# First feed-forward layer: silu on ScalarE instead of tanh there and a finishing product on VectorE

## The chip, the core and the metric

The kernel runs on one core of one Trainium2 chip, as one launch. The metric is the device time in microseconds of that core. The core's engines are TensorE (PE in the profile; PEld is its loading of weights), VectorE (DVE), ScalarE (ACT), GpSimd (POOL) and SyncE (SP), each with its own instruction stream. They wait for each other through semaphores. PSUM is the memory that TensorE writes its products to, in banks of 128 partitions by 512 fp32 numbers.

## The reference, cut to what matters

The input x has 4 sequences of 1024 tokens with 256 features. Six layers are applied in turn, each added to x:

```
x = x + 0.5 * L0_ffn(layernorm(x))
x = x + L0_attn(layernorm(x))
x = x + 0.5 * L0_ffn(layernorm(x))      # the same weights again
x = x + 0.5 * L1_ffn(layernorm(x))      # a mixture of experts
x = x + L1_attn(layernorm(x))
x = x + 0.5 * L1_ffn(layernorm(x))

def L0_ffn(x):                           # wq_*: whole numbers, s_*: one scale per row
    gate = silu(x @ ((wq_gate - 128) * s_gate[:, None]).T)     # 256 -> 704
    up   =      x @ ((wq_up   - 128) * s_up[:, None]).T        # 256 -> 704
    return (gate * up) @ ((wq_down - 128) * s_down[:, None]).T # 704 -> 256
```

silu(g) is g / (1 + exp(-g)), which is the same as 0.5 g (1 + tanh(g / 2)). The change touches `L0_ffn` alone, which runs twice.

## The kernel before, in words

The program is a row of phases, one function each: `prepare_phase` loads and turns the weights of the first layer, `ffn0_phase` ("f1_") is the first feed-forward layer, `attention_phase` ("a2_") the first attention, `ffn0_phase` ("f3_") the feed-forward layer again, and then come `mixture_phase`, `attention_phase` and `mixture_phase` once more. Between two phases there is a barrier of all engines: each engine enters the next block when all have left the one before.

`ffn0_phase` works through 8 chunks c of 512 tokens (4 tiles of 128). The hidden 704 features are 6 blocks j: five of 128 and a last one, j = 5, of 64. The gate and the up product of a block go to PSUM tiles `gate` and `up` with two banks each; block n = 6c + j uses bank j % 2, so block n can begin only when block n - 2 has let go of the bank. In the last block both halves fit into one bank: one group of four matmuls with the weights `ctT` gives the gate's 64 rows on partitions 0 to 63 of the gate's bank and the up product's 64 rows on partitions 64 to 127.

Inputs and hidden values are split into a high and a low fp16 part (`xh`, `xl`, and `hh`, `hl`), so each product is two fp16 matmuls. What each engine does, in the order in which it is written:

- TensorE: `gate_up(c, j)` (line 385) is 4 gate matmuls of 512 columns and then 4 up matmuls, all recorded on line 395. Behind block 1 stands `turn(c + 1)`, 8 transposes of the next chunk's normalised x, and behind each of blocks 1 to 4 one `down_proj(c - 1, i)`, 12 matmuls of 256 columns (line 407), which need all six `hl` of the chunk before. `gate_up` waits before its first gate matmul for `h_ready` of block n - 2, that is until VectorE has written `hT` of that block; with j = 0 it also waits for `xT_ready` of its chunk.
- ScalarE: `tanh(c, j)` (line 454, recorded on line 459) reads the gate's bank and writes tanh of half the scaled gate to `silu`. Then `upper_part(c, j - 1)` (line 452) copies `hT` of the block before to fp16 `hh`. Behind block 2 stands `keep_xT(c + 1)`, two copies to `xh` (line 447).
- VectorE: `gated(c, j)` (line 504, recorded on 507) makes `silu2` = (silu + 1) * gate, reading the gate's bank again. `hidden(c, j)` (line 510, recorded on 517) makes `hT` = silu2 * scale * up. In the last block the up rows are read from the gate's bank. The trace gives `silu2` the name `f_silu` as well. Between these stand the pieces of the work for the other chunks: the means (lines 487, 490, 493) and the normalising (501) of chunk c + 2, `lower_part` (524) for `xl` of chunk c + 1, `residual` (531) for the down product of chunk c - 1, `statistics` (536), which waits until GpSimd has added that tile to x, and `aggregate` (540).
- GpSimd: `add(c - 1, i)` (line 427) adds the finished tile to x, and `hl` = hT - hh (line 435) follows for every block. `hidden` of block n waits until `hl` of block n - 2 is written, since `hT` has two buffers.

In the names of the trace the first letter is the phase's, `f_` for both feed-forward phases. At the end of the phase the last chunk's four `down_proj` follow with nothing beside them.

## Time and profile before

| | |
|---|---|
| median of 3 runs | 2764.04 us (2758.51 to 2764.95) |
| the profiled execution | 2757.35 us, of which its span is 2755.6 us |
| TensorE, VectorE, ScalarE, GpSimd busy | 2581.0, 1872.7, 1269.7, 788.3 us |
| first feed-forward phase, first gate matmul to the last down matmul's end | 42.95 to 190.25 us of the span |
| second feed-forward phase, the same | 1142.47 to 1292.85 us |

The span runs from the first to the last instruction of the profiled execution; 1.75 us of the execution lie around it. Busy time is the time in which at least one instruction of the engine was under way. TensorE is busy 94% of the span, but a busy share is a mean over phases with different limits, so the change is read from the two feed-forward phases alone. Matmuls overlap: one of 512 columns is recorded with 0.38 us at the full clock while the next starts 0.22 us after it. So what a wait costs is read from start to start.

### The profile page before, as it was taken

How to read it: one execution, taken by the hardware profiler on the slowest of the kernel's cores; microseconds unless marked ns; L12 is line 12 of the kernel's file. 1: busy time of each engine (PE TensorE's matmuls, PEld its weight loads, DVE VectorE, ACT ScalarE, POOL GpSimd, SP SyncE). 2: the span in 40 equal slices, each digit the busy share in tenths (PEclk: the TensorE clock that was granted, in tenths of full speed). 3: DMA queues.
4: the chain of work that ended last, by engine and by line, in shares of the span. 5: the costliest groups of instructions: out<-in, count | busy, mean ns of one | idle time of the engine just before them, and what ended most of it. 6: DMA issues, size and time to landing. Idle time of an engine off the chain costs nothing. (4 is left out here: it accounts for less than half of the span.)

```text
span 2755.6 us, 38804 instructions
## 1 busy us (share of the span) xinstructions
PE 2581.0 (94%) x14106; PEld 1255.9 (46%) x14106; DVE 1872.7 (68%) x4022; ACT 1269.7 (46%) x1936; POOL 788.3 (29%) x760
## 2 busy tenths in 40 slices
PE   5987999999999999897999998899999999899998
PEld 3543333333333332354565665445544554555665
DVE  7868888788787885585664335787777776466334
ACT  4431666566566667543212322365454556321321
POOL 2545214132141300155424541311121110234441
PEclk8997999999999999899999999999999999999999
DMA  4004430331303400001303654634223440311565
GB/s 126 1 17 92 64 52 19 58 56 21 58 24 53 64 1 2 1 1 55 109 20 101 158 119 114 118 50 71 48 54 57 65 59 2 115 35 35 139 156 161
DMA packets 162592, 175.76 MB, mean 64 GB/s; under 512 B 19090, under 2 KB 135762, under 8 KB 162258
## 3 DMA queue, kind: packets, MB, share of 16 engines
q1 hardware_dynamic: 146948, 152.57, 25.4%
q0 software_dynamic: 12416, 17.84, 3.9%
q10 hardware_dynamic: 3040, 2.88, 0.4%
q8 instruction: 113, 1.85, 0.3%
q14 instruction: 75, 0.61, 0.1%
HBM read 116.32 MB, written 56.13 MB: 63 GB/s over the span
## 5 line engine op out<-in xcount | busy, mean ns | idle before, releaser
L1862 DVE TENSOR_REDUCE a_mx<-a_bank 128x1 f32<-128x512 f32 (+3 forms) x1792 | 1034.6, 626 | 241.7 <-PE a_bank L1595 173.1
L1730 ACT ACTIVATE a_E<-a_bank 128x1024 f32<-128x1024 f32 (+3 forms) x896 | 796.2, 931 | 401.5 <-PE a_bank L1653 273.7
L1595 PE MATMUL a_bank<-a_KT,a_QT 96*128 96x512 bf16 (+4 forms) x1792 | 572.3, 368 | 25.6 <-DVE a_mx L1862 15.2
L1653 PE MATMUL a_bank<-a_QT,a_KT 99*128 99x512 bf16 (+4 forms) x1792 | 505.1, 357 | 3.9 <-DMA a_QT<-a_mT 1.8
L1668 PE MATMUL a_bank<-a_E,a_Vg 128*32 128x512 f32 (+3 forms) x3584 | 437.3, 560 | 0.7 <-ACT a_E L1730 0.7
L1595 PEld LDWEIGHTS a_bank<-a_KT,a_QT 96*128 96x128 bf16 (+1 forms) x1792 | 152.0, 98 | 490.1 <-DVE a_mx L1862 307.5
L1653 PEld LDWEIGHTS a_bank<-a_QT,a_KT 99*128 99x128 bf16 (+1 forms) x1792 | 169.6, 98 | 173.5 <-ACT a_E L1730 31.4
L435 POOL TENSOR_TENSOR f_hl<-f_hT,f_hh 128x512 f16<-128x512 f32 x96 | 110.9, 1156 | 340.3 <-ACT f_hh L452 340.3
L903 PE MATMUL d_bank<-wdT,d_hT 128*128 128x256 f32 (+1 forms) x768 | 192.4, 393 | 4.2 <-DVE d_hT L1100 4.2
L1014 ACT ACTIVATE d_silu<-d_bank 128x512 f32<-128x512 f32 x96 | 57.1, 595 | 270.0 <-PE d_bank L888 270.0
L903 PEld LDWEIGHTS d_bank<-wdT,d_hT 128*128 128x128 f32 (+1 forms) x768 | 140.2, 191 | 63.2 <-issue 43.6
L888 PE MATMUL d_bank<-d_xT,wgT 128*128 128x512 f32 x320 | 162.6, 632 | 4.4 <-DMA wdT<-in_L_ffn_sw_down 4.4
L780 POOL DMA_INDIRECT acc<-d_ys,d_index x64 | 101.2, 1582 | 192.9 <-DVE d_ys L1216 119.6
L888 PE MATMUL d_bank<-d_xT,wuT 128*128 128x512 f32 x320 | 152.4, 599 | 0.0
L1530 POOL TENSOR_TENSOR a_Z<-a_Z,a_turns 128x512 f32<-128x512 f32 x24 | 30.5, 1270 | 414.6 <-DVE a_R L1811 414.6
L1668 PEld LDWEIGHTS a_bank<-a_E,a_Vg 128*32 128x32 f32 x3584 | 70.7, 108 | 139.9 <-issue 120.2
L1095 DVE SCALAR_TENSOR_TENSOR d_silu<-d_silu,d_bank 128x512 f32<-128x512 f32 x96 | 65.3, 680 | 98.9 <-ACT d_silu L1014 98.9
L1618 PE MATMUL a_bank<-a_xT,wqkvT 128*128 128x512 f32 x256 | 125.1, 621 | 2.0 <-DVE a_mx L1862 2.0
L790 POOL TENSOR_SCALAR d_xn<-x,mv,d_both 128x256 f32<-128x256 f32 x48 | 60.0, 1258 | 229.0 <-DVE d_shift L1237 150.8
L1108 DVE SCALAR_TENSOR_TENSOR x<-d_bank,d_hgate,x 128x256 f32<-128x256 f32 x64 | 30.9, 484 | 121.2 <-PE d_bank L903 121.1
L1598 PE MATMUL a_bank<-a_masks,ident_b 128*128 128x128 bf16 x512 | 112.3, 222 | 0.0
L459 ACT ACTIVATE f_silu<-f_gate,hscale 128x512 f32<-128x512 f32 x96 | 64.4, 683 | 103.8 <-PE f_gate L395 103.8
(235 smaller groups left out, 3633.9 us busy)
## 6 DMA issues: line engine op xcount, KB each, us to landing
parts<-a_parts SPq DMA_DIRECT2D x64, 384.0 KB, 2.6
a_QT<-parts SPq DMA_DIRECT2D x180, 128.0 KB, 5.9
a_KT<-parts SPq DMA_DIRECT2D x180, 128.0 KB, 9.1
d_wgu<-in_L_ffn_w_gate SPq DMA_DIRECT2D x64, 176.0 KB
d_wgu<-in_L_ffn_w_up SPq DMA_DIRECT2D x64, 176.0 KB
d_wd<-in_L_ffn_w_down SPq DMA_DIRECT2D x64, 176.0 KB
normalised<-d_xn SPq DMA_DIRECT2D x8, 1152.0 KB, 4.7
acc<-d_zero SPq DMA_DIRECT2D x2, 4224.0 KB, 16.4
```

What stands on the lines that cost most here:

```text
L435: nc.gpsimd.tensor_tensor(hl[0:r, c % 2, j, :], hT[0:r, j % 2, :], hh[0:r, c % 2, j, :], ALU.subtract).then_inc(hl_ready, 1)
L780: nc.gpsimd.indirect_dma_start(out=acc, out_offset=bass.IndirectOffsetOnAxis(ap=index[:, e:e + 1], axis=0), in_=ys[:, e % 2, :], in_offset ...
L888: last = nc.tensor.matmul(out, w[:, k, cols], xT[:, k, c * CW:(c + 1) * CW], start=(k == 0), stop=(k == KC - 1))
L903: last = nc.tensor.matmul(bank[:, down_bank(c, i), 0:D], hT[0:r, c % 2, j, i * P:(i + 1) * P], core.wdT[0:r, j, :], start=(j == 0), stop=( ...
L1095: nc.vector.scalar_tensor_tensor(out=silu2[0:r, j % 2, :], in0=silu[0:r, j % 2, :], scalar=1.0, in1=bank[0:r, acc_bank(n), :], op0=ALU.add ...
L1595: last = nc.tensor.matmul(out[:, 0:w], QT[0:W, h, qt * P:(qt + 1) * P], KT[0:W, h, kh * HALF:kh * HALF + w], start=True, stop=not diag)
L1598: last = nc.tensor.matmul(out[:, w - P:w], ident_b[:], masks[:, 0, :], start=False, stop=True)
L1618: last = nc.tensor.matmul(out, core.wqkvT[:, k, cols], xT[:, k, half * HALF:(half + 1) * HALF], start=(k == 0), stop=(k == KC - 1))
L1653: last = nc.tensor.matmul(out, KT[:, h, kt * P:(kt + 1) * P], QT[:, h, half * HALF + c0:(half + 1) * HALF], start=True, stop=not diag)
L1668: last = nc.tensor.matmul(bank[VW * j:VW * (j + 1), 4, c0:HALF], Vg[:, G % NG, kt, VS * j:VS * j + VW], E[:, u % 2, j, c0:HALF], start=fir ...
L1730: nc.scalar.activation(E[:, u % 2, 2 * pair:2 * pair + 2, c0:HALF], bank[:, 2 * pair:2 * pair + 2, c0:HALF], ACT.Exp).then_inc(exps, 1)
L1862: nc.vector.tensor_reduce(mx[:, x[1] // C % 2, j, qt, kh:kh + 1], out[:, 0:w], AX.X, ALU.max).then_inc(freed_dve, 1)
```

## The change

ScalarE no longer computes tanh of half the gate. It computes silu of the whole gate, with the scale that the weights ask for, and writes it to the same tile. VectorE's `gated` goes, with its tile `silu2` and its semaphore. What was `tanh` on ScalarE is now called `gated`, and `hidden` multiplies silu, up and one scale. The scales prepared once in `prepare_phase` change with that.

On TensorE the wait is moved and split. Before its gate matmuls a block waited for VectorE to have written `hT` of block n - 2. Now the gate matmuls wait for ScalarE to have read the gate's bank (`silu_ready` of block n - 2), and the up matmuls for `h_ready` of block n - 2. For j = 1, where block n - 2 is the last block of the chunk before and has its up rows in the gate's bank, the gate matmuls still wait for `h_ready`.

```diff
--- before.py
+++ after.py
@@ -295,9 +295,8 @@
                 statistics(1)
                 dve.wait_ge(s_in, 16 * 4)
                 for r, j in ((P, slice(0, FB - 1)), (hid(FB - 1), slice(FB - 1, FB))):
-                    nc.vector.tensor_scalar(core.hscale[0:r, j, 0], sg[0:r, j], 0.5 / LIFT, None, ALU.mult)
-                    nc.vector.scalar_tensor_tensor(out=core.hscale[0:r, j, 1], in0=sg[0:r, j], scalar=HLIFT / LIFT ** 2,
-                                                   in1=su[0:r, j], op0=ALU.mult, op1=ALU.mult).then_inc(scaled, 1)
+                    nc.vector.tensor_scalar(core.hscale[0:r, j, 0], sg[0:r, j], 1.0 / LIFT, None, ALU.mult)
+                    nc.vector.tensor_scalar(core.hscale[0:r, j, 1], su[0:r, j], 2.0 * HLIFT / LIFT, None, ALU.mult).then_inc(scaled, 1)
                 dve.wait_ge(r_in, START + 16 * 3)
                 nc.vector.tensor_tensor(prod[:], srows[:, 0], srows[:, 1], ALU.mult).then_inc(scaled, 1)
                 dve.wait_ge(scaled, START + 3)
@@ -351,7 +350,6 @@
         xh = sb(tag + "xh", [P, 2, KC, CW], F16)
         xl = sb(tag + "xl", [P, 2, KC, CW], F16)
         silu = sb(tag + "silu", [P, 2, CW])
-        silu2 = sb(tag + "silu2", [P, 2, CW])
         hT = sb(tag + "hT", [P, 2, CW])
         hh = sb(tag + "hh", [P, 2, FB, CW], F16)
         hl = sb(tag + "hl", [P, 2, FB, CW], F16)
@@ -363,8 +361,8 @@
         gate = ps(tag + "gate", [P, 2, CW])
         up = ps(tag + "up", [P, 2, CW])
         down = ps(tag + "down", [P, 2, 512])
-        names = ("root scales normed turned xh_ready xT_ready gate_s up_s silu_s silu2_s h hh_s hl_s down_s out_s x_done stats meaned")
-        (root, scales, normed, turned, xh_ready, xT_ready, gate_ready, up_ready, silu_ready, silu2_s, h_ready, hh_ready, hl_ready, down_ready,
+        names = ("root scales normed turned xh_ready xT_ready gate_s up_s silu_s h hh_s hl_s down_s out_s x_done stats meaned")
+        (root, scales, normed, turned, xh_ready, xT_ready, gate_ready, up_ready, silu_ready, h_ready, hh_ready, hl_ready, down_ready,
          out_s, x_done, stats, meaned) = (sem(tag + n) for n in names.split())
         ident = core.const("ident")
 
@@ -386,10 +384,13 @@
                     n, s = c * FB + j, c % 2
                     if j == 0:
                         pe.wait_ge(xT_ready, START + c * 2 + 2)
-                    if n > 1:
-                        pe.wait_ge(h_ready, START + n - 1)
                     for w, acc in ((core.cgT, gate), (core.cuT, up)) if j < FB - 1 else ((core.ctT, gate),):
                         cols = slice(j * P, (j + 1) * P) if j < FB - 1 else slice(0, P)
+                        if n > 1:
+                            if acc is gate and j != 1:
+                                pe.wait_ge(silu_ready, START + n - 1)
+                            else:
+                                pe.wait_ge(h_ready, START + n - 1)
                         for k in range(KC):
                             for part in (xh, xl):
                                 last = nc.tensor.matmul(acc[:, j % 2, :], w[:, k, cols], part[:, s, k, :],
@@ -451,18 +452,18 @@
                     act.wait_ge(h_ready, START + c * FB + j + 1)
                     nc.scalar.activation(hh[0:r, c % 2, j, :], hT[0:r, j % 2, :], ACT.Copy).then_inc(hh_ready, 1)
 
-                def tanh(c, j):
+                def gated(c, j):
                     n, r = c * FB + j, hid(j)
                     act.wait_ge(gate_ready, START + n + 1)
                     if n > 1:
                         act.wait_ge(h_ready, START + n - 1)
-                    nc.scalar.activation(silu[0:r, j % 2, :], gate[0:r, j % 2, :], ACT.Tanh,
+                    nc.scalar.activation(silu[0:r, j % 2, :], gate[0:r, j % 2, :], ACT.Silu,
                                          scale=core.hscale[0:r, j, 0:1]).then_inc(silu_ready, 1)
 
                 keep_xT(0)
                 for c in range(NCH):
                     for j in range(FB):
-                        tanh(c, j)
+                        gated(c, j)
                         if j:
                             upper_part(c, j - 1)
                         if j == 2 and c + 1 < NCH:
@@ -501,20 +502,14 @@
                     nc.vector.tensor_scalar(xn[:, i, :], core.x[:, t, :], mean[:, i:i + 1],
                                             core.rstd[:, t:t + 1], ALU.subtract, ALU.mult).then_inc(normed, 1)
 
-                def gated(c, j):
+                def hidden(c, j):
                     n, r = c * FB + j, hid(j)
                     dve.wait_ge(silu_ready, START + n + 1)
-                    nc.vector.scalar_tensor_tensor(out=silu2[0:r, j % 2, :], in0=silu[0:r, j % 2, :], scalar=1.0,
-                                                   in1=gate[0:r, j % 2, :], op0=ALU.add, op1=ALU.mult).then_inc(silu2_s, 1)
-
-                def hidden(c, j):
-                    n, r = c * FB + j, hid(j)
-                    dve.wait_ge(silu2_s, START + n + 1)
                     if j < FB - 1:
                         dve.wait_ge(up_ready, START + c * (FB - 1) + j + 1)
                     if n > 1:
                         dve.wait_ge(hl_ready, START + n - 1)
-                    nc.vector.scalar_tensor_tensor(out=hT[0:r, j % 2, :], in0=silu2[0:r, j % 2, :], scalar=core.hscale[0:r, j, 1:2],
+                    nc.vector.scalar_tensor_tensor(out=hT[0:r, j % 2, :], in0=silu[0:r, j % 2, :], scalar=core.hscale[0:r, j, 1:2],
                                                    in1=up[:, j % 2, :] if j < FB - 1 else gate[FR:P, j % 2, :],
                                                    op0=ALU.mult, op1=ALU.mult).then_inc(h_ready, 1)
 
@@ -553,7 +548,6 @@
                 for c in range(NCH):
                     more = c + 2 < NCH
                     for j in range(FB):
-                        gated(c, j)
                         if more and j <= 1:
                             mean_step(c + 2, j)
                         if j >= 2 and c:
```

What this does on VectorE is shown at the passage from one chunk to the next, from `hidden` of a chunk's last block (`64x512`) to `hidden` of the next chunk's second block. Before:

```order
L536 BN_STATS f_bn<-x 128x6 [waits f1_x_done]
L517 SCALAR_TENSOR_TENSOR f_hT<-f_silu,hscale,f_gate 64x512 [waits f1_hl_s,f1_silu2_s]
L501 TENSOR_SCALAR f_xn<-x,f_mean,rstd 128x256
L540 BN_AGGR mv<-f_bn 128x2 [waits f1_stats] x4
L507 SCALAR_TENSOR_TENSOR f_silu<-f_silu,f_gate 128x512 [waits f1_silu_s]
L487 TENSOR_REDUCE f_sums<-x 128x64 [waits f1_normed]
L517 SCALAR_TENSOR_TENSOR f_hT<-f_silu,hscale,f_up 128x512 [waits f1_hl_s,f1_up_s,f1_silu2_s]
L507 SCALAR_TENSOR_TENSOR f_silu<-f_silu,f_gate 128x512 [waits f1_silu_s]
L490 TENSOR_REDUCE f_mean<-f_sums 128x4 [waits f1_meaned]
L517 SCALAR_TENSOR_TENSOR f_hT<-f_silu,hscale,f_up 128x512 [waits f1_hl_s,f1_up_s,f1_silu2_s]
```

The same stretch of VectorE's stream after the change:

```order
L531 BN_STATS f_bn<-x 128x6 [waits f1_x_done]
L512 SCALAR_TENSOR_TENSOR f_hT<-f_silu,hscale,f_gate 64x512 [waits f1_hl_s,f1_silu_s]
L502 TENSOR_SCALAR f_xn<-x,f_mean,rstd 128x256
L535 BN_AGGR mv<-f_bn 128x2 [waits f1_stats] x4
L488 TENSOR_REDUCE f_sums<-x 128x64 [waits f1_normed]
L512 SCALAR_TENSOR_TENSOR f_hT<-f_silu,hscale,f_up 128x512 [waits f1_hl_s,f1_up_s,f1_silu_s]
L491 TENSOR_REDUCE f_mean<-f_sums 128x4 [waits f1_meaned]
L512 SCALAR_TENSOR_TENSOR f_hT<-f_silu,hscale,f_up 128x512 [waits f1_hl_s,f1_up_s,f1_silu_s]
```

Both rows on line 507 are gone, and nothing else has changed its place; line 512 now waits for ScalarE's semaphore directly. On TensorE the order of the matmuls is the same and only waits move. The passage into chunk 1, before, from the last matmul of block 5 (`ctT`) to the first gate matmul of block 1:

```order
L395 MATMUL f_gate<-f_xl,ctT 128x512
L395 MATMUL f_gate<-f_xh,cgT 128x512 [waits f1_h,f1_xT_ready]
L395 MATMUL f_gate<-f_xl,cgT 128x512
L395 MATMUL f_gate<-f_xh,cgT 128x512
L395 MATMUL f_gate<-f_xl,cgT 128x512
L395 MATMUL f_up<-f_xh,cuT 128x512
L395 MATMUL f_up<-f_xl,cuT 128x512
L395 MATMUL f_up<-f_xh,cuT 128x512
L395 MATMUL f_up<-f_xl,cuT 128x512
L395 MATMUL f_gate<-f_xh,cgT 128x512 [waits f1_h]
```

The same passage after:

```order
L396 MATMUL f_gate<-f_xl,ctT 128x512
L396 MATMUL f_gate<-f_xh,cgT 128x512 [waits f1_silu_s,f1_xT_ready]
L396 MATMUL f_gate<-f_xl,cgT 128x512
L396 MATMUL f_gate<-f_xh,cgT 128x512
L396 MATMUL f_gate<-f_xl,cgT 128x512
L396 MATMUL f_up<-f_xh,cuT 128x512 [waits f1_h]
L396 MATMUL f_up<-f_xl,cuT 128x512
L396 MATMUL f_up<-f_xh,cuT 128x512
L396 MATMUL f_up<-f_xl,cuT 128x512
L396 MATMUL f_gate<-f_xh,cgT 128x512 [waits f1_h]
```

The wait for `f1_h` has moved from the gate to the up matmuls at j = 0, and stands where it stood at j = 1. ScalarE's order and its number of table loads are as before.

## Rows read from the trace of the kernel before

**Rows 1.** Busy time, share and instructions of each engine, from the page.
```profile
PE 2581.0 (94%) x14106; PEld 1255.9 (46%) x14106; DVE 1872.7 (68%) x4022; ACT 1269.7 (46%) x1936; POOL 788.3 (29%) x760
```

**Rows 2.** Windows, one chunk: PE, PEld, DVE, ACT, POOL busy (instructions), clock, DMA.
```profile
93.90:111.40 17.50, 16.62 (x100) 9.15 (x100) 15.25 (x34) 8.20 (x15) 9.80 (x10) 1.00 0.01 1
```

**Rows 3.** TensorE's waits, 38 to 195 us: in total, times, longest.
```profile
PE f_gate L395 <- DVE f_hT L517: 7.3, 7, 2.0
PE f_down L407 <- POOL f_hl L435: 4.5, 1, 4.5
```

**Rows 4.** Timeline of TensorE into chunk 4: start, us, instruction, idle before.
```profile
107.58 0.27 PE L407 MATMUL f_down<-cdT,f_hl 64*128 64x256 f16 x1
...
108.44 0.38 PE L395 MATMUL f_gate<-f_xl,ctT 128*128 128x512 f16 x1
...
110.16 0.38 PE L395 MATMUL f_up<-f_xl,cuT 128*128 128x512 f16 x1
111.42 0.39 PE L395 MATMUL f_gate<-f_xh,cgT 128*128 128x512 f16 x1 [0.88 <-DVE f_hT L517]
```

**Rows 5.** Timeline of ScalarE, same place.
```profile
108.85 0.68 ACT L459 ACTIVATE f_silu<-f_gate,hscale 64x512 f32<-64x512 f32 x1 [2.04 <-PE f_gate L395]
```

**Rows 6.** Timeline of VectorE, same place.
```profile
106.52 0.67 DVE L507 SCALAR_TENSOR_TENSOR f_silu<-f_silu,f_gate 128x512 f32<-128x512 f32 x1
...
107.45 0.73 DVE L517 SCALAR_TENSOR_TENSOR f_hT<-f_silu,hscale,f_up 128x512 f32<-128x512 f32 x1
...
108.42 0.41 DVE L531 TENSOR_TENSOR f_out<-f_down,oscale 128x256 f32<-128x256 f32 x1
109.57 0.68 DVE L507 SCALAR_TENSOR_TENSOR f_silu<-f_silu,f_gate 64x512 f32<-64x512 f32 x1 [0.73 <-ACT f_silu L459]
110.17 0.41 DVE L536 BATCH_NORM_STATS2 f_bn<-x 128x6 f32<-128x256 f32 x1
110.61 0.75 DVE L517 SCALAR_TENSOR_TENSOR f_hT<-f_silu,hscale,f_gate 64x512 f32<-64x512 f32 x1
```

**Rows 7.** Timeline of GpSimd, same place.
```profile
108.92 0.73 POOL L427 TENSOR_TENSOR x<-f_out,x 128x256 f32<-128x256 f32 x1 [0.87 <-DVE f_out L531]
```

**Rows 8.** Timeline of TensorE into chunk 1.
```profile
54.80 0.38 PE L395 MATMUL f_gate<-f_xl,ctT 128*128 128x512 f16 x1
57.20 0.38 PE L395 MATMUL f_gate<-f_xh,cgT 128*128 128x512 f16 x1 [2.02 <-DVE f_hT L517]
```

**Rows 9.** Timeline of VectorE ahead of it.
```profile
52.61 0.69 DVE L507 SCALAR_TENSOR_TENSOR f_silu<-f_silu,f_gate 128x512 f32<-128x512 f32 x1 [0.20 <-ACT f_silu L459]
53.34 0.75 DVE L517 SCALAR_TENSOR_TENSOR f_hT<-f_silu,hscale,f_up 128x512 f32<-128x512 f32 x1
...
54.40 1.27 DVE L524 TENSOR_TENSOR f_xl<-f_tp,f_xh 128x512 f16<-128x512 f32 x2
...
56.30 0.75 DVE L517 SCALAR_TENSOR_TENSOR f_hT<-f_silu,hscale,f_up 128x512 f32<-128x512 f32 x1
```

**Rows 10.** Timeline of ScalarE, last block of the phase.
```profile
178.15 0.68 ACT L459 ACTIVATE f_silu<-f_gate,hscale 64x512 f32<-64x512 f32 x1 [2.04 <-PE f_gate L395]
```

**Rows 11.** Timeline of GpSimd, last two blocks of the phase.
```profile
179.43 1.15 POOL L435 TENSOR_TENSOR f_hl<-f_hT,f_hh 128x512 f16<-128x512 f32 x1 [1.00 <-ACT f_hh L452]
181.40 1.14 POOL L435 TENSOR_TENSOR f_hl<-f_hT,f_hh 64x512 f16<-64x512 f32 x1 [0.82 <-ACT f_hh L452]
```

**Rows 12.** Groups of ScalarE, whole span: busy, mean ns, idle before.
```profile
L459 ACT ACTIVATE f_silu<-f_gate,hscale 128x512 f32<-128x512 f32 x96 | 64.4, 683 | 103.8 <-PE f_gate L395 103.8
...
L1014 ACT ACTIVATE d_silu<-d_bank 128x512 f32<-128x512 f32 x96 | 57.1, 595 | 270.0 <-PE d_bank L888 270.0
...
L459 ACT ACT_TABLE_LOAD x2 | 2.6, 1283 | 0.0
```

**Rows 13.** Windows of the second phase, into its chunk 1; columns as in 2.
```profile
1155.30:1158.70 3.40, 1.38 (x7) 0.49 (x6) 3.37 (x7) 1.74 (x3) 1.18 (x2) 1.00 0.00 0
1158.70:1162.10 3.40, 3.40 (x10) 1.24 (x9) 2.44 (x5) 1.22 (x3) 2.30 (x2) 0.50 0.00 0
```

## The prediction

> **What bounds the kernel now.** I started at the page's shares: TensorE is busy 94% of the span and VectorE 68% [rows 1]. That is a mean over seven phases, so next I cut the first feed-forward phase into windows of one chunk. A chunk takes 17.50 us, TensorE is busy 16.62 of them, VectorE 15.25, ScalarE 8.20, GpSimd 9.80, at the full clock, 2.4 GHz [rows 2]. The reader is to see two engines close together: TensorE bounds, and VectorE is near enough to hold it up somewhere. Where, the list of TensorE's waits tells: seven waits for `hT`, 7.3 us with a longest of 2.0, and one of 4.5 us for `hl` at the phase's end [rows 3]. The second phase (1135 to 1300 us) has the same two entries with the same numbers. Then the timeline of the waits: six of the seven are alike, one at the head of block 1 of each of chunks 2 to 7. There two matmuls start at 110.16 and 111.42 [rows 4], 1.26 us apart where 0.22 is usual, so each costs 1.04 us. The seventh, the longest, is at the head of chunk 1: starts at 54.80 and 57.20 [rows 8].
>
> **The six waits of 1.04 us.** Gate matmuls of block 1 wait until `hT` of the chunk before's last block is written, since that reads the gate's bank. This wait stays as it is; what changes is how early `hT` comes. Now: the last `ctT` matmul starts at 108.44 and ends at 108.82 [rows 4], tanh runs 108.85 to 109.53 [rows 5], `gated` starts at 109.57, statistics at 110.17, `hidden` at 110.61 to 111.36 [rows 6], and TensorE goes on at 111.42.
>
> After: without `gated`, `hidden` can start at 109.57, if VectorE has the statistics behind it. These wait for GpSimd's add, that for the residual, that for the down product. The down product ends at 107.58 + 0.27 = 107.85 [rows 4]. The residual starts at 108.42 only because VectorE is late: the `gated` at 106.52 takes 0.6 us of its queue and `hidden` at 107.45 stands behind it [rows 6]. With that gone the residual starts at about 107.89 and ends at 108.30; GpSimd's add, which now starts 0.09 after the residual's end and takes 0.73 [rows 6, 7], ends at 109.12; statistics take 0.41, to about 109.57. `hidden` starts at 109.57 to 109.60, ends at 110.35, and TensorE may start at 110.41. Its own stream would reach that matmul at 110.16 + 0.22 = 110.38. The two meet within 0.03 us. I take 1.01 us gained of 1.04, six times: 6.1 us a phase. What is late next is TensorE itself, with this chain right behind it, so a chunk should take 16.5 us. Bounds: nothing is left of the wait (6.2), or GpSimd, statistics or the weight load behind the semaphore come 0.2 us later than I put them (5.0).
>
> VectorE loses six instructions of 683 ns spaced about 0.6 us, some 3.6 us of its 15.25 in a chunk, so it has 11.6 us of work in 16.5. `hidden` moves earlier, and with it `hh` and `hl`; ScalarE and GpSimd keep their loads and were not full.
>
> **The wait at chunk 1.** The last `ctT` matmul starts at 54.80, the next gate matmul at 57.20 [rows 8]. It waits for two things: `xl` of chunk 1 (two instructions from 54.40, together 1.27 us) and `hT` of block 4, from 56.30 to 57.05 [rows 9]. The second wait is moved: the gate's matmuls then wait for ScalarE alone, which has read block 4's gate by about 54.0. What is late next is `xl`. Ahead of it, `hidden` stands behind `gated` at 52.61 and starts at 53.34 [rows 9]; now it starts when silu is there, at 52.61, so all behind it comes 0.73 earlier and `xl` is done at 54.94. Gate matmuls start at 54.99 instead of 57.20: 2.2 us. The up matmuls, due at 54.99 + 0.87 = 55.86, need `hT` of block 4, which comes at about 55.6 (0.73 earlier, and one more `gated` less, 0.7). Block 1, due at 56.72, needs `hT` of block 5: its silu is done at 55.69, VectorE is through with `hidden` of block 4 and one normalise at about 55.9, so `hT` is there at 56.65 to 56.7. Nothing or up to 0.3 us is left there. I take 2.2 us a phase, with bounds of 1.9 and 2.4 (the whole start-to-start gap of 2.40 less 0.22, and another 0.2 ahead of the `ctT` matmuls, which now also wait for `hT`).
>
> **The end of the phase.** The last four down products wait for the last `hl`. Now tanh starts at 178.15 and takes 0.68 [rows 10], and the last `hl` runs from 181.40 [rows 11]. After, `hidden` follows silu at 178.87 and ends at 179.62, `hh` takes 0.63 and ends at about 180.28. But `hl` of block 4 runs on GpSimd from 179.43 for 1.15 us [rows 11]; it doesn't come earlier, since its `hh` stands behind the last silu on ScalarE. So the last `hl` starts at about 180.56 instead of 181.40: 0.84 us, not the 1.04 that the chain would give. GpSimd is the next in line there.
>
> **The clock.** In the second phase the stretch with the wait at chunk 1 (TensorE busy 1.38 of 3.40 us) is followed by one at a clock of 0.50, that is 1.2 GHz, in which TensorE is busy throughout [rows 13]. At half the clock those 3.40 us do the work of 1.70, so the drop costs up to 1.7 us. In the first phase the same wait is followed by the full clock. If the wait goes, so should this drop: 0 to 1.7 us. The warm-up at the phase's start and the drop at its end stay, and where they fall moves with the phase, which can give or take about as much. I take 0.7 us.
>
> **ScalarE.** It runs as many activations as before, at the same places in its queue. What silu takes no row shows. The nearest rows are tanh with the same tile, source and scale, 683 ns, and tanh without a scale tensor, 595 ns [rows 12]. I take 683. Lower brings nothing, since TensorE bounds. Above, I bound it by twice the row, 1366 ns, as if it were worked out in two passes. The Trainium skill ("ScalarE: Activation LUTs", the six pipelined stages) says that all functions cost the same per element, 0.833 ns, and names only a switch of tables as dearer. No row here shows silu, and by that rule the sum stays what it is. The two scales of `prepare_phase` are made by four instructions before and after, on at most 5 columns: nothing.
>
> **The sum.** A phase gives 6.1 + 2.2 + 0.84 = 9.1 us, two give 18.2, with the clock 18.9. Between the phases stand barriers and semaphores, no fixed times, and the loads of the next phase are issued behind its barrier, so all that follows moves up by as much. The profiled execution took 2757.35 us, so a like one would take 2738.4. The median of the runs shown is 2764.04, 6.7 above it; the predicted time goes by the median: 2764.04 - 18.9 = 2745.1 us. A difference under about 0.3%, 8.3 us, can't be told from none here.
>
> **Rivals.**
> *The wait stays in part (faster, less so).* Block 1 still waits for `hT`, and the tie of 110.41 against 110.38 hangs on four hand-overs between engines. If each chunk keeps 0.4 us, 12 times, 4.8 us are lost: a gain of 14, 2750. For it: the tie itself, and that the first weights can't be loaded ahead. Against: the durations repeat to 0.02 us from chunk to chunk.
>
> *The change does not do what it says at the place that counts.* The bank of the one block that waits is not released by ScalarE. If the statistics held `hidden` back as now (the residual not earlier), the 1.04 us would shrink to 0.5 only, and with `xl` late as well at chunk 1 the gain is 2 x (3.2 + 0.7 + 0.4) = 8.6 or less: 2755 or more, at the edge of no change. Against: the residual's operand has been there since 107.85.
>
> *Silu takes twice the row.* Each hand-over at 109.53 comes 0.68 later: six times 0.36 are gained, about 0.8 at chunk 1, 0.15 at the end, 3.1 a phase: 2758, within 0.3%.
>
> *Slower: ScalarE becomes the bound.* Place: the same chain, and then ScalarE's queue. At 683 + 1040 ns for silu all six waits are back; from there each further ns is lost once a chunk. ScalarE's 8.20 us a chunk grow by six times the surplus and pass the old 17.50 when silu takes about 2.2 us. At 2.7 us (four times the row) a chunk takes some 20.3 us, 2.8 x 8 x 2 = 45 us lost: 2809. Nothing in the profile speaks for it: the two kinds of activation in rows 12 lie at 0.60 and 0.68 us.
>
> The same side could come from table loads. Line 459 has one a phase, 1283 ns [rows 12]. If silu's table lacked the plain copy, ScalarE would load ten times a chunk, 12.8 us on top of 8.2: 21.0, so 56 us slower, 2820. In the changed stream ScalarE has one load ahead of the first silu and none between silu and copies. The Trainium skill ("ScalarE: Activation LUTs", the hidden batching unit) says that cheap functions such as copy are in every set and that a function outside the active set needs a load; by that rule too, one load a phase stays.
>
> **Chances and range.** Forecast 0.80; wait stays in part 0.08; not earlier at the place that counts 0.04; silu doubled 0.04; slower by ScalarE 0.04, of which a quarter for the tables. So faster 0.88, within 0.3% 0.08, slower 0.04. The forecast's own range is 2745 less 6, the spread of the three runs and a gain of 20 to 22, and plus 8, a gain of 15 with the same spread: 2739 to 2753. To leave out no more than 2 in 10, runs as quick as the profiled one and the second rival are taken in: 2734 to 2757.
>
> **What would show it.** Right: line 507's group gone; silu x96 at 683 ns; TensorE's seven waits for `hT` under 1 us in all; a chunk of 16.5 us; the chunk-1 gate matmul waiting for `xl` (line 519), if for anything; the final wait for `hl` 3.6 us, with GpSimd without idle before it. Wrong: ScalarE's silu over 0.75 us, the block-1 gap over 0.5 us, or a chunk still at 17 us with TensorE idle elsewhere; or phases shorter by 9 us and other phases longer.

## The result, and the profile after

| | before | changed | ratio, 95% interval |
|---|---|---|---|
| median | 2761.28 us (2755.56 to 2764.95, 4 runs) | 2739.05 us (2738.51 to 2740.84, 4 runs) | 0.9932, 0.9911 to 0.9953 |
| profiled execution; span | 2757.35; 2755.6 us | 2740.84; 2739.0 us | |
| first feed-forward phase, start of the first gate matmul to start of the last down matmul | 147.03 us | 140.67 us | |
| second, the same | 150.11 us | 140.21 us | |
| a chunk, from the first transpose to that of the next | 17.50 us | 16.71 us | |

The kernel became faster by 0.7%. The median lies inside the wide range of the prediction (2734 to 2757 us) and at the low end of the forecast's own (2739 to 2753). The two profiled spans differ by 16.6 us: 6.4 and 9.9 in the two phases and 0.3 elsewhere. The medians differ by 22.2, but the four runs of before spread over 9.4 us, so the sum of the prediction is checked against the spans. There 16.6 us stand against the forecast 18.9.

The page's busy times answer to [rows 1]; VectorE has 96 instructions and 31 us less, TensorE the same work:

```profile
PE 2578.6 (94%) x14106; PEld 1256.2 (46%) x14106; DVE 1841.4 (67%) x3926; ACT 1269.8 (46%) x1936; POOL 788.9 (29%) x760
```

One chunk as in [rows 2], now 16.71 us long. TensorE is busy 16.62 us of it as before; only its idle time went:

```profile
93.62:110.33 16.71, 16.62 (x101) 9.15 (x100) 13.54 (x28) 8.21 (x15) 9.78 (x11) 1.00 0.01 1
```

VectorE fell by 1.71 us here, from 15.25 to 13.54. Six instructions spaced 0.6 us are gone, which is 3.6. So something else on VectorE has grown.

TensorE's waits in the first phase (us in total, times, longest), to set against [rows 3]:

```profile
PE f_down L408 <- POOL f_hl L436: 3.6, 1, 3.6
PE f_gate L396 <- DVE f_xl L519: 2.4, 2, 1.6
```

The seven waits for `hT` are gone from the list, and the wait at chunk 1 is now one for `xl` (0.8 of the 2.4; the other 1.6 stands at the phase's start, as before). Shorter gaps don't appear in it, because a matmul of 0.38 us still covers them. They show in the starts. TensorE into chunk 4, as [rows 4] (`...` marks rows left out):

```profile
105.54 0.27 PE L408 MATMUL f_down<-cdT,f_hl 64*128 64x256 f16 x1
...
106.40 0.38 PE L396 MATMUL f_gate<-f_xl,ctT 128*128 128x512 f16 x1
...
108.13 0.38 PE L396 MATMUL f_up<-f_xl,cuT 128*128 128x512 f16 x1
108.60 0.39 PE L396 MATMUL f_gate<-f_xh,cgT 128*128 128x512 f16 x1
```

From 108.13 to 108.60 are 0.47 us where 0.22 is usual. Of the 1.04 us per chunk, 0.25 is left; I had forecast 0.03. VectorE, ScalarE and GpSimd at the same place, as [rows 5 to 7]:

```profile
104.70 0.72 DVE L512 SCALAR_TENSOR_TENSOR f_hT<-f_silu,hscale,f_up 128x512 f32<-128x512 f32 x1
105.35 0.82 DVE L502 TENSOR_SCALAR f_xn<-x,f_mean,rstd 128x256 f32<-128x256 f32 x1
106.08 0.41 DVE L526 TENSOR_TENSOR f_out<-f_down,oscale 128x256 f32<-128x256 f32 x1
107.34 0.43 DVE L531 BATCH_NORM_STATS2 f_bn<-x 128x6 f32<-128x256 f32 x1 [0.84 <-POOL x L428]
107.80 0.75 DVE L512 SCALAR_TENSOR_TENSOR f_hT<-f_silu,hscale,f_gate 64x512 f32<-64x512 f32 x1
```

```profile
106.82 0.68 ACT L460 ACTIVATE f_silu<-f_gate,hscale 64x512 f32<-64x512 f32 x1 [2.04 <-PE f_gate L396]
```

```profile
104.86 1.16 POOL L436 TENSOR_TENSOR f_hl<-f_hT,f_hh 128x512 f16<-128x512 f32 x1 [0.81 <-ACT f_hh L453]
106.58 0.73 POOL L428 TENSOR_TENSOR x<-f_out,x 128x256 f32<-128x256 f32 x1 [0.56 <-DVE f_out L526]
```

Silu is there at 106.82 + 0.68 = 107.50, but `hidden` starts at 107.80, behind the statistics. These wait for the add, the add for the residual, and the residual starts at 106.08 though its down product ended at 105.81. Ahead of it stands normalise, which takes 0.82 us. In the kernel before it took 0.41. The group of normalise in the first phase, before and after (busy us, mean ns):

```profile
L501 DVE TENSOR_SCALAR f_xn<-x,f_mean,rstd 128x256 f32<-128x256 f32 x32 | 12.7, 412 | 0.2
```

```profile
L502 DVE TENSOR_SCALAR f_xn<-x,f_mean,rstd 128x256 f32<-128x256 f32 x32 | 25.2, 803 | 0.1
```

The same instruction, untouched by the change, takes twice as long: 12.5 us of VectorE a phase. Over both phases of the changed kernel 46 of its 64 instances start beside a GpSimd instruction that has at least 0.15 us still to run, and take 0.95 us in the mean; the other 18 take 0.41. Before, 6 of 64 started so, and they took 0.43 to 0.48.

The trace of before shows the same effect at another instruction, in nearly every chunk. The last of the mean steps, a tensor_scalar of 128x4, takes 0.16 us with nothing on GpSimd beside it. In 12 of its 16 instances `hl` was under way, and then it took 0.62 (once 0.36) and ended about 0.03 after `hl`. VectorE alone and beside `hl`, then GpSimd, all in the kernel before:

```profile
42.81 0.16 DVE L493 TENSOR_SCALAR f_mean<-f_mean 128x4 f32<-128x4 f32 x1
98.90 0.62 DVE L493 TENSOR_SCALAR f_mean<-f_mean 128x4 f32<-128x4 f32 x1
```

```profile
98.34 1.16 POOL L435 TENSOR_TENSOR f_hl<-f_hT,f_hh 128x512 f16<-128x512 f32 x1 [2.59 <-ACT f_hh L452]
```

So the effect could have been read before the change, from one instruction whose duration differs from place to place.

Where ScalarE's groups stand against [rows 12], silu takes what tanh took, and the table loads are two as before:

```profile
L460 ACT ACTIVATE f_silu<-f_gate,hscale 128x512 f32<-128x512 f32 x96 | 64.2, 683 | 110.3 <-PE f_gate L396 110.3
...
L460 ACT ACT_TABLE_LOAD x2 | 2.6, 1283 | 0.0
```

The passage into chunk 1 [rows 8, 9] on TensorE, VectorE and GpSimd:

```profile
55.54 0.38 PE L396 MATMUL f_gate<-f_xl,ctT 128*128 128x512 f16 x1
56.70 0.39 PE L396 MATMUL f_gate<-f_xh,cgT 128*128 128x512 f16 x1 [0.78 <-DVE f_xl L519]
```

```profile
53.57 0.75 DVE L512 SCALAR_TENSOR_TENSOR f_hT<-f_silu,hscale,f_up 128x512 f32<-128x512 f32 x1 [0.21 <-ACT f_silu L460]
54.24 1.21 DVE L502 TENSOR_SCALAR f_xn<-x,f_mean,rstd 128x256 f32<-128x256 f32 x1
55.37 1.28 DVE L519 TENSOR_TENSOR f_xl<-f_tp,f_xh 128x512 f16<-128x512 f32 x2
56.56 0.73 DVE L512 SCALAR_TENSOR_TENSOR f_hT<-f_silu,hscale,f_up 128x512 f32<-128x512 f32 x1
```

```profile
54.14 1.16 POOL L436 TENSOR_TENSOR f_hl<-f_hT,f_hh 128x512 f16<-128x512 f32 x1 [0.92 <-ACT f_hh L453]
```

Here normalise takes 1.21 us: it starts 0.10 after `hl` and ends 0.15 after it. `xl` comes that much later.

### The profile page after: what moved, and what is told of

It is laid out like the page before. It is cut to its first block and busy times, and to the rows that moved or that the text cites. A ratio compares the mean times of both kernels' runs of the same rounds, so it can differ in the third digit from the quotient of the medians.

```text
span 2739.0 us, 38708 instructions
## 1 busy us (share of the span) xinstructions
PE 2578.6 (94%) x14106; PEld 1256.2 (46%) x14106; DVE 1841.4 (67%) x3926; ACT 1269.8 (46%) x1936; POOL 788.9 (29%) x760
```

## The experiments

Theory A: VectorE's normalise is held until the GpSimd instruction beside it has ended. The change, by moving `hidden` forward, put normalise beside `hl`, and that took back part of the gain. Theory B: the hand-overs between the engines are slower than I put them. Behind the two profiled kernels of the table, the first four ran beside each other on one chip, the next four on a second, the next two on a third and the last on a fourth, each with runs of before beside them, to which the ratios go. Chunk lengths, gaps (from start to start, 0.22 is usual) and normalise's mean in the first phase come from each kernel's trace; the runs behind one median scatter over 5 to 14 us, so the medians tell only whether a kernel is faster than before, and the traces alone tell the variants apart. "Gap at block 1" is that of chunks 2 to 6, and the gaps are those of the first phase.

| kernel | median us | ratio to before, 95% | chunk us | gap at block 1 | gap at chunk 1 | normalise ns |
|---|---|---|---|---|---|---|
| before (profile) | | | 17.50 | 1.26 | 2.40 | 412 |
| changed (profile) | 2739.05 | 0.9932 (0.9911 to 0.9953) | 16.71 | 0.47 | 1.16 | 803 |
| normalise in another form | 2744.39 | 0.9946 (0.9934 to 0.9958) | 16.85 | 0.61 | 1.29 | 895 |
| residual first | 2741.92 | 0.9936 (0.9923 to 0.9948) | 16.59 | 0.35 | 1.16 | 571 |
| before, normalise in another form | 2762.32 | 1.0007 (0.9995 to 1.0018) | 17.50 | 1.26 | 2.54 | 488 |
| silu only | 2746.00 | 0.9951 (0.9938 to 0.9964) | 16.71 | 0.47 | 1.89 | 803 |
| changed, again | 2741.01 | 0.9943 (0.9929 to 0.9957) | 16.71 | 0.46 | 1.15 | 803 |
| `hl` in halves | 2740.56 | 0.9942 (0.9928 to 0.9956) | 16.49 | 0.25 | 0.66 | 519 |
| split wait only, on before | 2755.94 | 1.0002 (0.9993 to 1.0012) | 17.50 | 1.26 | 1.83 | 412 |
| normalise on ScalarE | 2739.46 | 0.9935 (0.9921 to 0.9950) | 16.49 | 0.25 | 0.22 | 592, on ScalarE |
| halves in chunks 0 to 5 | 2739.65 | 0.9925 (0.9909 to 0.9941) | 16.49 | 0.25 | 0.66 | 518 |
| changed, third time | 2742.73 | 0.9938 (0.9922 to 0.9954) | 16.71 | 0.48 | 1.15 | 802 |
| accumulator out | 2741.52 | 0.9948 (0.9935 to 0.9960) | 16.49 | 0.25 | 0.50 | 532 |

**Normalise in another form.**

```diff
-nc.vector.tensor_scalar(xn[:, i, :], core.x[:, t, :], mean[:, i:i + 1],
-                        core.rstd[:, t:t + 1], ALU.subtract, ALU.mult)
+nc.vector.scalar_tensor_tensor(out=xn[:, i, :], in0=core.x[:, t, :], scalar=mean[:, i:i + 1],
+                               in1=core.rstd[:, t:t + 1].to_broadcast([P, D]), op0=ALU.subtract, op1=ALU.mult)
```

> The changed kernel, with VectorE's normalise (line 502, one tensor_scalar of 128x256) written as a scalar_tensor_tensor with the same operands. Theory A (normalise is held until GpSimd's hl, which runs beside it, is done; it took 803 ns in the mean after the change against 412 before): the new form, like hidden, is not held and takes 0.4 to 0.5 us; the residual of block 4 starts at the down product's end, the 0.47 us from start to start at block 1 falls to 0.22 to 0.25, a chunk takes 16.5 us for 16.71; at chunk 1 xl comes 0.7 us earlier. Together about 12 x 0.22 + 2 x 0.7 = 4 us faster than the changed kernel. Theory B (the hand-over between VectorE and GpSimd is slower than assumed, normalise has nothing to do with it): normalise may shorten but a chunk stays at 16.7 us, no gain.

My expectation failed: the new form is held too, 895 ns in the mean, and a chunk grew by 0.14 us. The normalise ahead of the late residual is no longer than before (0.81 for 0.82), but it ends 0.28 us after `hl`, where the old form ended 0.15 after it, and the residual starts 0.20 after `hl`'s end for 0.06. So a chunk follows the end of the held instruction. That speaks against theory B and leaves open what makes an instruction one that is held. VectorE's group, then VectorE and GpSimd at the one place:

```profile
L502 DVE SCALAR_TENSOR_TENSOR f_xn<-x,f_mean,rstd 128x256 f32<-128x256 f32 x32 | 28.1, 895 | 0.1
```

```profile
105.46 0.81 DVE L502 SCALAR_TENSOR_TENSOR f_xn<-x,f_mean,rstd 128x256 f32<-128x256 f32 x1
106.19 0.41 DVE L527 TENSOR_TENSOR f_out<-f_down,oscale 128x256 f32<-128x256 f32 x1
```

```profile
104.83 1.16 POOL L436 TENSOR_TENSOR f_hl<-f_hT,f_hh 128x512 f16<-128x512 f32 x1 [0.67 <-ACT f_hh L453]
```

**Residual first.** The lines of `normalise` and `residual` change places in the loop.

```diff
-if more and j >= 2:
-    normalise(c + 2, j - 2)
 if c and 1 <= j <= CT:
     residual(c - 1, j - 1)
+if more and j >= 2:
+    normalise(c + 2, j - 2)
```

> The changed kernel, with residual placed ahead of normalise in VectorE's order in each block. Theory A: normalise may still be held by GpSimd, but the residual no longer stands behind it, so a chunk takes 16.5 us for 16.71 and 12 x 0.22 = 2.6 us are gained; chunk 1 starts as in the changed kernel, since in chunk 0 there is no residual. Theory B: a chunk stays at 16.7 us, as the residual, the add and the statistics take what they take.

A chunk takes 16.59 us, half of the way to the 16.5 expected. Chunk 1 is unchanged, as expected. GpSimd's timeline shows where the other half is:

```profile
106.47 0.83 POOL L428 TENSOR_TENSOR x<-f_out,x 128x256 f32<-128x256 f32 x1 [0.34 <-DVE f_out L526]
```

The add takes 0.83 us where it took 0.73: now normalise starts first (106.31 to 106.72) and GpSimd is the one that is slowed. All 15 adds of the first phase that start during a normalise take 0.83, the other 17 take 0.73. In the run before this one, six `hl` of 64x512 that start during a normalise take 1.31 for 1.15. So the effect goes both ways, by who starts first. That GpSimd stands still until normalise has ended is not shown: normalise had 0.25 us to run, and the add is 0.10 longer.

**Before, normalise in another form.** The same diff as above on the kernel before.

> The kernel before, with normalise in the scalar_tensor_tensor form. Theory A: in the kernel before normalise ran between GpSimd's hl (412 ns in the mean), so the form gains nothing: same time within 1 us, each chunk 17.50 us. If the form itself were simply better for this program whatever stands beside it, this kernel would gain about 4 us too.

No gain, and 488 ns for normalise in a place where hardly any `hl` runs beside it. This is the form's own price: 0.08 us more than the old form.

**Silu only.** The gate matmuls wait for `hT` at every block, as before the change.

```diff
-if acc is gate and j != 1:
-    pe.wait_ge(silu_ready, START + n - 1)
-else:
-    pe.wait_ge(h_ready, START + n - 1)
+pe.wait_ge(h_ready, START + n - 1)
```

> The changed kernel, with TensorE's gate matmuls waiting for hT of block n-2 at every block, as before the change: silu on ScalarE and one VectorE instruction less, but no earlier release of the gate's bank. Theory A (the six waits of a phase went because VectorE has less to do; the moved wait matters at chunk 1 alone): a chunk stays at 16.71 us; at chunk 1 the gate matmul starts after hT of block 4, 0.6 us later than in the changed kernel, so 1.2 us slower than it in all. Rival (the bank given back by ScalarE is what helps): chunks go back towards 17.5 us, up to 9 us slower than the changed kernel.

As theory A had it: a chunk 16.71 us, and at chunk 1 a gap of 1.89 instead of 1.16, so the moved wait is worth 0.73 us a phase and nothing elsewhere. The two phases lose 1.5 us by it, where 1.2 was expected. The rest of the change, silu and one VectorE instruction less, gives all that remains of the gain.

**Split wait only, on before.** `pe.wait_ge(h_ready, ...)` for the gate becomes `pe.wait_ge(silu2_s, ...)` except at j = 1, the up matmuls get the wait for `hT`; the rest is the kernel before.

> The kernel before, with the wait of TensorE split alone: gate matmuls wait until VectorE's gated has read the bank, up matmuls for hT, block 1's gate matmuls for hT as before. Tanh and gated stay. Theory A (VectorE's load and its place in the chain set the time, not the bank's release): the six waits of 1.04 us stay; at chunk 1 the gate matmuls start at xl, about 1.5 us earlier, but the up matmuls and block 1 then wait for hT at the old times, so at most 0.2 us a phase is left: same time as before. Rival (the earlier release matters): up to 2 x 2.2 us faster than before.

Same time as before. At chunk 1 the gate matmuls start 0.57 us sooner (gap 1.83), and block 1 right behind has a new gap of 0.88, 0.66 over the usual one. They did not start at `xl`, 1.5 us sooner, as I expected: the last thing they wait for is `gated` of block 4, which reads the bank on VectorE.

```profile
57.37 0.38 PE L398 MATMUL f_gate<-f_xh,cgT 128*128 128x512 f16 x1 [1.45 <-DVE f_silu L510]
```

So the bank comes free 0.57 us earlier here, not as early as in the changed kernel, and even that gives nothing while VectorE is late with `hT`.

**The changed kernel, again.**

> The changed kernel itself, as the measure for the three beside it on the same chip. A chunk 16.71 us, normalise 0.80 us in the mean; about 17 to 20 us faster than before.

Its chunks and gaps repeat to within 0.02 us. Its median was 2741.01, and 2742.73 in a third set, where this was expected:

> The changed kernel once more, as the measure for the one beside it on the same chip: a chunk 16.71 us, about 17 to 20 us faster than before.

The chunk came as expected, the time did not. The medians of before beside them are 2755.45 (17 runs) and 2758.99 (11 runs), so the changed kernel is 14.4 and 16.3 us faster and not 17 to 20. These differences lie nearer to the 16.6 us of the two spans than the 22.2 of the first table do, which rest on four runs each.

**`hl` in halves.**

```diff
-nc.gpsimd.tensor_tensor(hl[0:r, c % 2, j, :], hT[0:r, j % 2, :], hh[0:r, c % 2, j, :], ALU.subtract).then_inc(hl_ready, 1)
+for half in (slice(0, CW // 2), slice(CW // 2, CW)):
+    last = nc.gpsimd.tensor_tensor(hl[0:r, c % 2, j, half], hT[0:r, j % 2, half], hh[0:r, c % 2, j, half], ALU.subtract)
+last.then_inc(hl_ready, 1)
```

> The changed kernel, with GpSimd's hl made by two instructions of 256 columns instead of one of 512. Theory A (VectorE's normalise, which reads and writes SBUF alone, is held until the GpSimd instruction beside it has ended, in either form): it is now held for at most about 0.6 us instead of 1.16, its mean falls from 0.80 to 0.5 to 0.6 us, the residual of block 4 is no longer late, a chunk takes 16.5 us for 16.71, and chunk 1 starts about 0.5 us earlier. Together 12 x 0.2 + 2 x 0.5 = 3.4 us faster than the changed kernel, less if the two halves take GpSimd clearly longer than 1.16 us. Theory C (the two slow each other down evenly for as long as both run): normalise stays near 0.8 us and so does the chunk.

This decides for theory A. Not a VectorE instruction is changed, GpSimd's `hl` becomes longer as a whole (1.35 for 1.16), and normalise falls from 803 to 519 ns in the mean of the first phase, with 0.67 to 0.72 where it starts beside the beginning of a half. VectorE at one place, then GpSimd:

```profile
103.28 0.52 DVE L504 TENSOR_SCALAR f_xn<-x,f_mean,rstd 128x256 f32<-128x256 f32 x1
103.97 0.42 DVE L528 TENSOR_TENSOR f_out<-f_down,oscale 128x256 f32<-128x256 f32 x1 [0.17 <-PE f_down L408]
```

```profile
102.98 1.35 POOL L437 TENSOR_TENSOR f_hl<-f_hT,f_hh 128x256 f16<-128x256 f32 x2 [1.03 <-ACT f_hh L455]
```

The residual waits for its down product and no longer behind normalise, and the chunk is at 16.49 us, the forecast 16.5. Theory C, an even slowing of both, falls as well. The longer `hl` costs 0.28 us each at the last chunk's first down product and at the phase's end. By the traces that leaves 1.0 us a phase and 2.1 in all, where 3.4 was expected with the proviso of a longer `hl`; the medians, 2740.56 and 2741.01, can't show it.

**Normalise on ScalarE.** VectorE's mean step makes -mean * rstd, and for chunks 2 to 7 ScalarE normalises.

The line added on ScalarE (the diff is cut to it):

```diff
+nc.scalar.activation(xn[:, i, :], core.x[:, t, :], ACT.Identity, scale=core.rstd[:, t:t + 1],
+                     bias=mean[:, i:i + 1]).then_inc(normed, 1)     # two tiles behind blocks 3 and 4
```

> The changed kernel, with the normalising of chunks 2 to 7 moved to ScalarE (x times rstd plus a bias, two tiles each behind blocks 3 and 4); the mean step on VectorE makes the bias. Theory A: nothing on VectorE is held by GpSimd ahead of the residual or of xl, so block 1 starts with the usual 0.22 to 0.28, a chunk takes 16.46 to 16.5 us, and in chunk 0 xl follows hidden of block 3 directly: chunk 1 starts without a wait, 0.9 us earlier a phase. Together 10 x 0.25 + 2 x 0.9 = 4.3 us faster than the changed kernel. Rival (ScalarE, 8.2 us a chunk, becomes late with 2.4 us more, or is itself slowed by GpSimd): silu or hh come later and new waits of TensorE appear.

The chunk is at 16.49 us as expected. On ScalarE normalise takes 0.59 to 0.61 us in all 24 instances of the first phase, beside `hl` or not, so ScalarE is not slowed by GpSimd. The gain at chunk 1 was not had: its gate matmuls start without a gap, but block 1 of chunk 1 then waits with a gap of 1.23 for `hT`, since the last silu of chunk 0 stands behind two normalises on ScalarE. The rival named was right at that one place. By the traces 1.05 us a phase and 2.1 in all are gained on the changed kernel, where 4.3 was expected.

```profile
57.04 0.75 DVE L524 SCALAR_TENSOR_TENSOR f_hT<-f_silu,hscale,f_gate 64x512 f32<-64x512 f32 x1 [1.31 <-ACT f_silu L460]
```

**Halves in chunks 0 to 5.** The loop over halves as above where `c + 2 < NCH`, else the whole.

> The changed kernel, with hl in two halves in chunks 0 to 5 alone, where a normalise stands beside it, and in one instruction in chunks 6 and 7. Theory A: chunks at 16.49 us and a shorter wait at chunk 1 as with halves throughout (1.6 us a phase less than the changed kernel), while the final wait for hl goes back from 4.29 to 4.01 us from start to start, and the wait at the head of the last chunk's first down product from 0.80 to 0.52. Together 3.3 us faster than the changed kernel, 1.1 faster than halves throughout. If a chunk with whole hl is no longer late only because of the halves before it, the two gains do not add.

Both gains add: chunks 16.49, chunk 1 at 0.66, the last chunk's two gaps back at 0.52 and 4.01. By the traces that is 1.1 us for the chunks and 0.5 at chunk 1, 1.6 a phase and 3.2 in all, less than the changed kernel. The medians, 2739.65 and 2742.73 beside each other, lie the same way, but each set spreads over 5 to 8 us. No measured time here tells the two kernels apart.

**Accumulator out.**

```diff
 nc.vector.tensor_scalar(xn[:, i, :], core.x[:, t, :], mean[:, i:i + 1],
-                        core.rstd[:, t:t + 1], ALU.subtract, ALU.mult)
+                        core.rstd[:, t:t + 1], ALU.subtract, ALU.mult, accum_out=unused[:, i:i + 1])
```

> The changed kernel, with normalise still a tensor_scalar of 128x256 with one SBUF input, but asked to write its accumulator to a spare tile too. The Trainium skill (SBUF - State Buffer, Who interferes with whom) says that this form does not enter the two-port mode, and that an instruction with one SBUF input outside that mode does not contend with GpSimd. Theory A as sharpened by that (normalise is held because it takes the port pair that it shares with GpSimd): 0.5 to 0.6 us, the same whether hl runs beside it or not, a chunk 16.46 to 16.52 us, the start-to-start gap at chunk 1 at most 0.7 for 1.15: 3 to 4 us faster than the changed kernel. Rival (any VectorE instruction that reads and writes SBUF alone is held by GpSimd): it is held as before, 0.8 us in the mean or more, a chunk 16.7 us or longer.

The values that this form writes are not the normalised x; it is run for its time alone. Normalise takes 526 to 535 ns in all 24 instances of the first phase's chunks 2 to 7, beside `hl` or not. VectorE here, and the `hl` beside it:

```profile
105.10 0.53 DVE L503 TENSOR_SCALAR_CACHE_REDUCE f_xn<-x,f_mean,rstd 128x256 f32<-128x256 f32 x1
105.56 0.08 DVE L503 DVE_READ_ACCUMULATOR f_xn<-x,f_mean,rstd 128x1 f32 x1
105.79 0.42 DVE L528 TENSOR_TENSOR f_out<-f_down,oscale 128x256 f32<-128x256 f32 x1 [0.15 <-PE f_down L409]
```

```profile
104.80 1.16 POOL L437 TENSOR_TENSOR f_hl<-f_hT,f_hh 128x512 f16<-128x512 f32 x1 [1.02 <-ACT f_hh L454]
```

It starts 0.30 us into an `hl` of 1.16 and isn't held. The chunk is 16.49 us and the gap at chunk 1 is 0.50, with one of 0.37 at block 1 behind it. So it isn't every SBUF instruction of VectorE that is held. By the traces the two phases are 3.3 us shorter than the changed kernel's, inside the 3 to 4 expected. The median doesn't show it: it lies 14.1 us below that of before beside it (2755.57), no more than the changed kernel's own 14.4 and 16.3.

## Why the prediction was right, and where its sum was off

| step, per phase | forecast | spans of before and changed |
|---|---|---|
| waits at block 1 of chunks 2 to 6 | 5 x 1.01 | 5 x 0.79 |
| the same at chunk 7 | 1.01 | 1.01 |
| chunk 1 | 2.2 | 1.44 |
| last chunk's first down product | 0 | -0.15 |
| end of the phase | 0.84 | 0.86 |
| sum | 9.1 | 7.1 |

- *The path.* TensorE was held by VectorE at seven places and by `hl` at one. The seven waits for `hT` went. At the six passages TensorE's own stream is now the limit to within 0.25 us; chunk 1 still waits, for `xl`, and the end for `hl`. The order of what is late next was right at chunk 1 (`xl`) and at the end (GpSimd, back to back from 174.19).
- *The six waits.* The mechanism held, the size was off by 0.22 us in five of six. Of 1.04 us a chunk 0.79 were gained; with that the phase's 4.96 lies just under my bounds of 5.0 to 6.2. The step that failed is the sentence that with `gated` gone the residual starts at the down product's end. What stands ahead of it did move, but between `hidden` and the residual stands a normalise that the prediction doesn't name, and so left at its 0.41 us. It grew to 0.82, because its new place lies beside `hl`. At the passage into chunk 7 no normalise stands there, since there are no chunks 8 and 9; TensorE's starts there are 158.28 and 158.53, so a gap of 0.25 and exactly the 0.03 forecast. Halves and the accumulator form bring the other chunks to that same 0.25. What happened is about half of the first rival, that the wait stays in part with 0.4 us a chunk. But it was not one of the four hand-overs that the rival names, and its counter-argument, that the durations repeat to 0.02 us from chunk to chunk, holds only as long as each instruction keeps its neighbours.
- *Chunk 1.* Forecast 2.2 with bounds of 1.9 and 2.4, found 1.44: the gap of 2.40 became 1.16, and 0.20 ahead of the `ctT` matmuls went as well. The failed step is the same one: normalise ahead of `xl` took 1.21 us in place of 0.48. With halves 0.5 us of it came back.
- *The moved wait* is worth 0.73 us a phase, at chunk 1 alone, and only together with the lighter VectorE.
- *Silu's price.* 683 ns, as taken. Both rivals on ScalarE fall, the tables too.
- *The clock.* I took 0.7 of 0 to 1.7. The drop in the second phase is gone; after the shorter wait the full clock follows, to set against [rows 13]:

```profile
1146.60:1150.00 3.40, 2.62 (x13) 1.04 (x12) 3.40 (x6) 2.08 (x4) 2.32 (x2) 1.00 0.00 0
1150.00:1153.40 3.40, 3.40 (x20) 1.71 (x18) 3.30 (x6) 2.42 (x4) 2.33 (x2) 1.00 0.00 0
```

  Of the four phases traced in the kernel before and in before with the other form of normalise two had the drop; of the 22 phases of the other eleven traces, with shorter gaps at chunk 1, none had. So that the profile of before held one drop is chance in part. The warm-up's place in the phases gave about 0.7 us more: the full clock came 3.0 and 6.0 us after the first gate matmul before, 4.3 and 3.4 after, and each us at half the clock costs half. So 2 x 7.1 = 14.2 from the steps, 1.7 for the drop and 0.7 for the warm-up make 16.6; the last four down products, part of them at half the clock before and after, took 0.06 and 0.15 us longer, and the two phases together became 16.3 us shorter.
- *The median.* The forecast 2745.1 stands 6 above the measured 2739.05. I had added 6.7 us because the median of before lay above its profiled execution. That was scatter of before, and the changed kernel's runs did not have it. The gain that I took too large (18.9 for 16.6) and the addition that should not have been made (6.7) partly cancel. That is luck: with the right gain the forecast would have stood 8 above and not 6. The range of 2734 to 2757 holds the median either way.

## What to carry to other kernels

A duration read from a trace belongs to its neighbours too. When an instruction is moved earlier, ask what then runs beside it on GpSimd, and let VectorE's tensor_scalar and scalar_tensor_tensor from SBUF to SBUF end only behind that neighbour. Look in the trace of before for an instruction whose duration differs from place to place. An earlier release of a buffer is worth something only where the other thing that the same stretch needs is early as well; one part of a change can be worth nothing alone (here the split wait) and something beside the other, so test them apart. And a gap shorter than a matmul is in no list of waits: compare the starts.

## What the runs showed of the hardware that I had not expected

VectorE's tensor_scalar of 128x256 fp32 from SBUF to SBUF takes 0.41 us alone and up to 1.21 beside a GpSimd tensor_tensor of 1.16 us, ending about 0.15 us after it. One of 128x4 takes 0.16 alone and up to 0.88, ending 0.03 after it. The scalar_tensor_tensor with both tensors in SBUF is held in the same way (0.48 alone, up to 1.34, ending 0.28 after it). In the other order GpSimd is slowed: its add took 0.83 instead of 0.73. Not held, beside the same GpSimd instruction, were `hidden` and the residual, which read one operand from PSUM (0.75 and 0.42), the reduction to `sums` (1.19), the tensor_scalar that writes its accumulator (0.53), and ScalarE's normalise (0.59).

The Trainium skill (SBUF — State Buffer, "Who interferes with whom") says that the two engines share one pair of SBUF ports, that a VectorE instruction in a two-port mode, or with two SBUF inputs while GpSimd reads SBUF, contends for it, and that whoever issues first has it for the whole instruction while the other "fully blocks". The runs agree on which VectorE instructions are held and which are not, and that the order decides. By that rule alone normalise could not be done before `hl`, from 104.86 to 106.02, had ended; it ended at 106.17. The 0.15 us between are from these traces and not from the rule, and a normalise that began all its 0.41 us at 106.02 would have ended at 106.43. The rule speaks against this change at the one step where my sum failed, and I had not weighed it.
